# Sparse feed-forward: down product as three fp32r products, h turned earlier, weight splits dealt anew

## The reference

```python
h = silu(x @ w_gate) * (x @ w_up)          # x: 1024 x 256, h: 1024 x 1024
a = abs(h.reshape(B, S, I // 4, 4))
_, idx = top_k(a, 2)                       # of each four neighbours the two largest stay
h_sparse = h * mask
x = x + 0.5 * (h_sparse @ w_down)          # w_down: 1024 x 256
```

## Time and profile before

| | |
|---|---|
| median of 3 runs | 1663.79 us (1658.72 to 1665.37) |
| the profiled execution | 1661.38 us, span 1659.6 us |
| first sparse feed-forward | 793 to 893 us of the span |
| second sparse feed-forward | 1554 us to the end |
| PE busy, share of the span | 88% |
| DVE, ACT, POOL busy | 65%, 51%, 29% |
| mean granted TensorE clock | 0.938 of full speed |

### The profile page before, as it was taken

How to read it: one execution, slowest core, us unless ns; L and a number is a source line. 1 busy time by engine, 2 the same in 40 slices (tenths; PEclk the granted TensorE clock), 3 DMA queues, 4 the chain that set the end, 5 groups by cost and what they waited for, 6 DMA issues and landing times. The chain is left out here.

```text
span 1659.6 us, 24358 instructions
## 1 busy us (share of the span) xinstructions
PE 1454.4 (88%) x7712; PEld 1014.0 (61%) x7712; DVE 1085.8 (65%) x1948; ACT 847.5 (51%) x1206; POOL 487.5 (29%) x407
## 2 busy tenths in 40 slices
PE   3999589999999976997697887899999999998697
PEld 2566443333333344664486776788887887887586
DVE  4122499999999843121676766787877778877475
ACT  1222227777777731221433767576666675765332
POOL 1344220000000112443100104756655656565100
PEclk7999769999999976999799989999999999999799
DMA  8522211111111028222201012222222222221200
GB/s 296 145 45 45 56 27 20 26 27 27 27 27 27 5 75 299 47 47 44 92 1 39 20 38 87 90 83 89 96 77 96 76 91 93 82 91 39 76 1 26
DMA packets 83007, 111.79 MB, mean 67 GB/s; under 512 B 11904, under 2 KB 60800, under 8 KB 82912
## 3 DMA queue, kind: packets, MB, share of 16 engines
q1 hardware_dynamic: 73152, 96.05, 19.3%
q0 software_dynamic: 9376, 14.16, 4.8%
q10 hardware_dynamic: 384, 0.39, 0.1%
HBM read 89.99 MB, written 11.93 MB: 61 GB/s over the span
## 5 line engine op out<-in xcount | busy, mean ns | idle before, releaser
L923 DVE TENSOR_REDUCE attn_max_chunks<-attn_scores 128x1 f32<-128x512 f32 x488 | 305.4, 684 | 22.9 <-PE attn_scores L1174 22.8
L1085 ACT ACTIVATE attn_probs<-attn_scoresT 128x1024 f32<-128x1024 f32 x256 | 248.0, 1022 | 111.9 <-PE attn_scoresT L1190 111.6
L1174 PE MATMUL attn_scores<-attn_k_picks,attn_q_group 64*128 64x512 f32 x488 | 185.8, 461 | 11.1 <-DVE attn_max_chunks L923 2.3
L1174 PEld LDWEIGHTS attn_scores<-attn_k_picks,attn_q_group 64*128 64x128 f32 x488 | 84.7, 189 | 172.6 <-DVE attn_max_chunks L923 163.9
L1605 DVE SCALAR_TENSOR_TENSOR ssm_scan_x<-ssm_scan_proj,ssm_w_conv,ssm_scan_x 128x1023 f32<-128x1023 f32 (+2 forms) x96 | 123.0, 1282 | 81.8 <-ACT ssm_scan_x L1600 75.4
L401 DVE TENSOR_TENSOR moe_h<-moe_silu,moe_up 128x512 f32<-128x512 f32 x46 | 31.6, 688 | 189.9 <-PE moe_up L516 189.9
L1190 PE MATMUL attn_scoresT<-attn_q_group,attn_k_picks 64*128 64x512 f32 x512 | 152.2, 435 | 3.2 <-ACT attn_probs L1085 3.2
L1202 PE MATMUL attn_o<-attn_probs,attn_v_group 128*32 128x512 f32 x1024 | 137.3, 608 | 0.4 <-ACT attn_probs L1085 0.3
L62 PE MATMUL ssm_scan_proj<-ssm_xnT_hi,ssm_w_in_hi 128*128 128x512 f32 x256 | 109.4, 427 | 23.7 <-DVE ssm_scan_x L1605 21.7
L448 ACT ACTIVATE moe_silu<-moe_gate 128x512 f32<-128x512 f32 x46 | 27.5, 598 | 200.9 <-PE moe_gate L516 200.9
L286 POOL DMA_INDIRECT moe_sums<-moe_y,moe_token x46 | 72.7, 1580 | 165.7 <-DVE moe_y L410 160.0
(11 more groups left out here) (339 smaller groups left out, 3092.4 us busy)
## 6 DMA issues: line engine op xcount, KB each, us to landing
ssm_cum_all<-ssm_cums SPq DMA_DIRECT2D x32, 512.0 KB, 3.8
...
moe_sums<-main_residual SPq DMA_DIRECT2D x2, 1024.0 KB, 5.6
```

Source lines behind the costliest of these rows:

```text
L923: return nc.vector.tensor_reduce(rmaxc[:, half, place:place + 1], chunk_bank(g, n), AX_X, ALU.max).then_inc(reduced, 1)
L1085: nc.scalar.activation(probs[s % 2][:, 2 * pair:2 * pair + 2, :], st_ps[pair][:], ACT.Exp, scale=SCALE).then_inc(exp_done, 1)
L1174: nc.tensor.matmul(chunk_bank(g, n), qs[b][head_rows(j), t * P:(t + 1) * P], kz[b][head_rows(j), j % 2, c * BANK:(c + 1) * BANK], start=Tr ...
```

## The change

`down` becomes `matmul3`: 24 fp32r matmuls of 256 columns for eight fp32 ones. ACT's copy of the transposed h becomes a cast to fp32r (`hT_hi`), and DVE subtracts two halves of 512 columns (`h_low`) to get `hT_lo`. PE's list becomes `gate(t, 0)`, `up(t, 0)`, `turn_x(t + 1)`, `gate(t, 1)`, `turn_h(t - 1)`, `up(t, 1)`, `down(t - 1)`. `w_down` is split in one piece: ACT casts it between the second silu and `magnitude` of tile 0, POOL then subtracts. Of the four parts of gate and up, gate 0 goes to DVE altogether (cast and subtraction); ACT casts the other three, POOL subtracts for gate 1, DVE for both of up.

```diff
@@ sparse_ffn_layer
+        w_dn_hi = sp.sb("w_down_hi", [P, KF, D], F32R)
+        w_dn_lo = sp.sb("w_down_lo", [P, KF, D], F32R)
-        hT = sp.sb("hT", [P, KF, P])
+        hT_hi = sp.sb("hT_hi", [P, KF, P], F32R)
+        hT_lo = sp.sb("hT_lo", [P, KF, P], F32R)
...
-            eng.wait_ge(w_hi_done, w_parts.index((n, c)) + 1)
+            if (n, c) == w_parts[0]:
+                eng.wait_ge(first_hi_done, 1)
+            else:
+                eng.wait_ge(w_hi_done, w_parts.index((n, c)))
...
         @block.gpsimd
         def _(pool):
-            for n, c in w_parts:
-                if n == "gate":
-                    split_low(pool, nc.gpsimd, n, c)
+            split_low(pool, nc.gpsimd, "gate", 1)
+            pool.wait_ge(down_loaded, 64)
+            pool.wait_ge(w_dn_hi_done, 1)
+            nc.gpsimd.tensor_tensor(w_dn_lo[:], w_dn[:], f32(w_dn_hi[:]), ALU.subtract).then_inc(w_dn_lo_done, 1)
...
+            def h_low(t, c):
+                dve.wait_ge(hT_hi_done, 2 * t + c + 1)
+                own = slice(4 * c, 4 * c + 4)
+                nc.vector.tensor_tensor(hT_lo[:, own, :], hT_ps[c][:], f32(hT_hi[:, own, :]), ALU.subtract).then_inc(hT_lo_done, 1)
+
             normalize(0)
             normalize(1)
             x_low(0)
+            for k in range(KD):
+                dve.wait_ge(loaded["gate", k], 16)
+                last = nc.vector.tensor_copy(in_places(w_hi["gate"], 0)[:, k], by_place(w_raw["gate"], 0)[:, k])
+            last.then_inc(first_hi_done, 1)
+            split_low(dve, nc.vector, "gate", 0)
             split_low(dve, nc.vector, "up", 0)
             split_low(dve, nc.vector, "up", 1)
             for t in range(TT):
                 if t:
                     sparsify(t - 1)
                 product(t, 0)
+                if t >= 2:
+                    add(t - 2)
+                if t:
+                    for c in range(2):
+                        h_low(t - 1, c)
+                product(t, 1)
                 if t < LAST:
                     x_low(t + 1)
-                if t >= 2:
-                    add(t - 2)
                 if t + 2 < TT:
                     normalize(t + 2)
-                product(t, 1)
             sparsify(LAST)
             add(LAST - 1)
+            for c in range(2):
+                h_low(LAST, c)
...
                 silu(t, 1)
+                if t == 0:
+                    act.wait_ge(down_loaded, 64)
+                    nc.scalar.copy(w_dn_hi[:], w_dn[:]).then_inc(w_dn_hi_done, 1)
+                else:
+                    turned(t - 1)
                 act.wait_ge(h_done, 2 * t + 2)
                 if t:
                     act.wait_ge(sparse, t)
                 nc.scalar.activation(mag[:], h[t % 2][:], ACT.Abs).then_inc(mag_done, 1)
-                if t:
-                    turned(t - 1)
...
             def down(t):
                 if t == 0:
-                    pe.wait_ge(down_loaded, 64)
+                    pe.wait_ge(w_dn_lo_done, 1)
                 else:
                     pe.wait_ge(added, t)
                 for k in range(KF):
                     if k % 4 == 0:
-                        pe.wait_ge(hT_done, 2 * t + k // 4 + 1)
-                    last = nc.tensor.matmul(out_ps[:], hT[:, k, :], w_dn[:, k, :], start=(k == 0), stop=(k == KF - 1))
+                        pe.wait_ge(hT_lo_done, 2 * t + k // 4 + 1)
+                    last = matmul3(nc, out_ps[:], (hT_hi[:, k, :], hT_lo[:, k, :]), (w_dn_hi[:, k, :], w_dn_lo[:, k, :]),
+                                   start=(k == 0), stop=(k == KF - 1))
                 last.then_inc(out_done, 1)
 
             turn_x(0)
             for t in range(TT):
-                ups(t, 0)
+                gate(t, 0)
+                up(t, 0)
                 if t < LAST:
                     turn_x(t + 1)
-                if t >= 2:
-                    down(t - 2)
-                ups(t, 1)
+                gate(t, 1)
                 if t:
                     turn_h(t - 1)
-            down(LAST - 1)
+                up(t, 1)
+                if t:
+                    down(t - 1)
             turn_h(LAST)
             down(LAST)
```

More of the change, by code:

```diff
@@ L1347, in sparse_ffn_layer @@
         w_parts = (("gate", 0), ("up", 0), ("gate", 1), ("up", 1))
+        first_hi_done = sp.sem("first_hi_done")
         loaded = {(n, k): sp.sem(f"{n}{k}_loaded") for n in src for k in range(KD)}
@@ L1350, in sparse_ffn_layer @@
         w_hi_done = sp.sem("w_hi_done")
-        w_lo_done = {n: sp.sem(f"w_{n}_lo_done") for n in src}
+        w_lo_done = {(n, c): sp.sem(f"w_{n}{c}_lo_done") for n, c in w_parts}
         eps_done, mv_done, std_done, rstd_done = (sp.sem(n) for n in ("eps_done", "mv_done", "std_done", "rstd_done"))
@@ L1375, in split_low @@
                                          f32(in_places(w_hi[n], c)[:, k]), ALU.subtract)
-            last.then_inc(w_lo_done[n], 1)
+            last.then_inc(w_lo_done[n, c], 1)
         @block.sync
@@ L1477, in split @@
             def split(n, c):
-                if c == 0:
+                if (n, c) in (("up", 0), ("gate", 1)):
                     for k in range(KD):
@@ L1497, in turned @@
                         act.wait_ge(out_done, t)
-                    nc.scalar.copy(hT[:, 4 * c:4 * c + 4, :], hT_ps[c][:]).then_inc(hT_done, 1)
+                    nc.scalar.copy(hT_hi[:, 4 * c:4 * c + 4, :], hT_ps[c][:]).then_inc(hT_hi_done, 1)
             def silu(t, c):
@@ L1506, in _ @@
             x_high(0)
-            for n, c in w_parts:
+            for n, c in w_parts[1:]:
                 split(n, c)
@@ L1530, in turn_x, with project, gate @@
                 last.then_inc(x_turned, 1)
-            def ups(t, c):
+            def project(n, t, c, bank):
                 b = t % 2
+                if t == 0:
+                    pe.wait_ge(w_lo_done[n, c], 1)
+                for k in range(KD):
+                    cols = slice(c * BANK, (c + 1) * BANK)
+                    last = matmul3(nc, bank[:], (xT_hi[b][:, k, :], xT_lo[b][:, k, :]),
+                                   (w_hi[n][:, k, cols], w_lo[n][:, k, cols]), start=(k == 0), stop=(k == KD - 1))
+                return last
+            def gate(t, c):
                 pe.wait_ge(x_lo_done, t + 1)
@@ L1536, in ups, with up @@
                     pe.wait_ge(silu_done, 2 * t - 1 + c)
+                project("gate", t, c, gate_ps[c]).then_inc(gate_done, 1)
+            def up(t, c):
+                if t:
                     pe.wait_ge(h_done, 2 * t - 1 + c)
-                for n, bank, done in (("gate", gate_ps[c], gate_done), ("up", up_ps[c], up_done)):
-                    if t == 0:
-                        pe.wait_ge(w_lo_done[n], c + 1)
-                    for k in range(KD):
-                        cols = slice(c * BANK, (c + 1) * BANK)
-                        last = matmul3(nc, bank[:], (xT_hi[b][:, k, :], xT_lo[b][:, k, :]),
-                                       (w_hi[n][:, k, cols], w_lo[n][:, k, cols]), start=(k == 0), stop=(k == KD - 1))
-                    last.then_inc(done, 1)
+                project("up", t, c, up_ps[c]).then_inc(up_done, 1)
             def turn_h(t):
@@ L1549, in turn_h @@
                 if t:
-                    pe.wait_ge(hT_done, 2 * t)
+                    pe.wait_ge(hT_lo_done, 2 * t)
                 flat = h[t % 2][:].rearrange("p w q -> p (w q)")
```

4 lines of the change are left out of this document (3 added, 1 removed).

## The result

The changed kernel takes 1685.95 us (median of 4 runs, 1683.94 to 1687.63) beside 1664.08 for the kernel before in the same job: ratio 1.0125, 95% interval 1.0109 to 1.0141. It is slower by more than the 0.5% that can be told apart. The forecast was 1675, its range 1665 to 1681: the direction was right, the size too small, and the time lies outside the range. The profiled execution took 1683.94 us, 22.56 more than the profiled one of before (1661.38).

A forecast was written before the change was run, and what follows sets the result against it. PE alone set the 10.06 us tile before; afterwards a chain through sparsify would, at 9.75. Terms of +0.6, +2.9 and +3.3 make +6.8 us a layer, +13.6 for both: 1661.4 to 1675 us, range 1665 to 1681.

The forecast's parts named there:

- chain: Steady tiles: second product, magnitudes, sparsify and turn of h wait on each other, 9.75 us a tile; +0.6 us a layer.
- start: POOL beside DVE, cast: First tile: POOL's w_down subtraction stretches sparsify(0) by 2.5 us, ACT's cast delays magnitudes by 0.43; +2.9 us a layer.
- clock at the first turn: PE idles 4.7 us ahead of the layer's first turn of h and its clock falls; +1.5 us charged.
- clock at the last turn: PE idles 4.45 us ahead of the layer's last turn of h, clock falls to 0.50; 1.8 us charged.
- end at full clock: Last sparse to last add: level at full clock, down(7) done at 4.9 us, last add at about 5.2 as before.
- S + 2.7: Steady tile: the second product starts 2.7 us after S, the end of the previous tile's sparsify.
- `sparsify(0)` keeps 5.2 us: First tile on DVE: a sign that the prediction is wrong; it expected sparsify(0) 1.5 to 3.8 us longer than the others.
- the +0.43 for the cast: Tile 0 on ACT: casting w_down behind the second silu starts the magnitudes at 813.07 instead of 812.64.
- how the numbers follow: Closing step: forecast 0.68, range 1665 to 1681; slower 0.63, within 0.5% 0.33, faster 0.04.
- The first: Rival: chain holds, but POOL hardly slows sparsify and PE's clock does not fall; +2 a layer, 1665 us; chance 0.24.
- The second: Rival: PE stays the bound, chain shorter by say 0.3 us, seven tiles of 9.5, no clock fall; 1658 us; chance 0.05.
- The third: Rival: weight loads do not hide behind down's 24 matmuls, 5.5 us a tile; +32, near 1695 us; chance 0.03.

The follow-up runs named there:

- e5: Changed kernel with POOL's long subtraction for w_down left out (low part zero but for 8 columns); 1674.05 us, ratio 1.0046 to the kernel before.
- e6: Changed kernel plus matmuls nobody reads, 12 ahead of PE's first turn of h and 18 ahead of the last; 1673.67 us, ratio 1.0035.
- e10: Changed kernel, unchanged, run again for a second profile and time; ratio 1.0119 to the kernel before.
- e8: Kernel before the change, unchanged, run again for a second profile; ratio 0.9996.
- e11: Changed kernel without POOL's long subtraction and with 18 matmuls nobody reads ahead of the last turn of h; 1667.96 us, ratio 1.0009.
- e1: Changed kernel with POOL's subtraction for w_down cut into eight instructions of 256 columns; 1683.13 us, ratio 1.0102 to the kernel before.
- e2: Changed kernel with normalize(2) moved ahead of the second product of tile 0; 1684.76 us, ratio 1.0107 to the kernel before.
- e7: Changed kernel with fp32r down later, behind the turn; fp32 down for tiles 6 and 7; w_down's low part on DVE in four pieces; 1666.56 us, ratio 1.0012.
- e9: The changed kernel reworked: fp32r down behind the turn for tiles 2 to 5 only, w_down's subtraction on DVE, add(5) inside the last sparsify; 1660.78 us, ratio 0.9971.
- e3: Changed kernel with down as eight fp32 matmuls again, no split of w_down and no h_low, new PE order kept; 1672.40 us, ratio 1.0045.
- e4: Changed kernel with the turn of h back behind the second half, fp32r down kept a tile later, two hT buffers, add moved; 1692.75 us, ratio 1.0162.

## Why the prediction was right or wrong

Per layer, first and second, forecast against what the first profiles show:

| term | forecast | measured | from |
|---|---|---|---|
| chain | +0.6 | +0.2, +0.1 | seven steps of e5 less before |
| start: POOL beside DVE, cast | +2.9 | +3.3, +3.3 | first `sparse`, after less before |
| clock at the first turn | +1.5 | +2.6, +1.6 | seven steps, after less e5 |
| clock at the last turn | +1.8 | +2.3, +1.8 | last `add`, after less e6 |
| end at full clock | 0 | +0.1, +0.1 | last `add`, e6 less before |
| sum | +6.8 | +8.5, +6.9 | table: +8.45, +6.95 |

The second profiles (e10 less e8) give 5.6 and 3.0 for the start, 1.8 and 1.9 for the seven steps, 1.9 and 1.9 for the last `add`.

**The direction, the chain and the two falls of the clock were right.** The steady step was forecast at 9.75 and is 9.69, the second product at S + 2.7 and is at S + 2.64, `down` at 2.86 and is 2.88, and the clock fell at both turns named. e5, e6 and e11 take terms away and find the rest as it was within 0.6 us. The mechanism of the start was not right, and by the prediction's own sign (`sparsify(0)` keeps 5.2 us) wrong.

**The chain** was sized too high, even under its lower bound of +0.5: 67.8 and not 68.25, from seven times 0.06 us.

**The start term was mis-sized, by a wrong mechanism.** I read 2.12 us for 1.22 us as a slowing by 1.73, took two thirds of it on account of gaps, and said that `sparsify(0)` would be the one stretched. It kept its 5.22 us in the first profile of after, with `normalize(2)` in its place. DVE is held, not slowed in proportion: the price is what is left of POOL's 4.6 us when the first SBUF-only instruction comes, less what idle time DVE had there. It came to 3.3 where +2.5 was charged, and 3.4 to 3.7 in `sparsify(0)` of e1 and e2; the +0.43 for the cast came to nothing (e5). Minimum, median and maximum in the earlier trace rows hid this. The row of POOL that overlaps the DVE row of 1105.37 there, in the trace of before, shows it:

```profile
1105.32 1.10 POOL L2118 TENSOR_SCALAR_AFFINE_SELECT ssm_cum_all<-ssm_cum_all 128x1024 f32<-128x1024 f32 x1
```

POOL ends at 1106.42 and DVE at 1107.49, 1.07 later, not much less than the 1.22 it takes alone; wherever L2225 overlaps L2118 in this trace the distance is 1.07 to 1.09.

**The clock term** was near where it was not cut: 1.8 at the last turn, which cost 1.8 in three of the four layers and 2.3 in one. At the first turn I charged 1.5, on the ground that part of the delay is slack of PE. After the turn PE had no slack, since the next product waits for up(1, 1); it cost 1.6 to 1.8 in three layers and 2.6 in the first of the first profile. The idle times were forecast at 4.7 and 4.45 us; they were 3.31 (and 1.37 a little earlier) and 4.33.

**The step that put the time outside the range** is the last one, how the numbers follow. The layers give 15.4 us (16.2 between the second profiles, e10 less e8), 1.8 to 2.6 over the forecast's 13.6, and that alone ends at 1677 from the profiled 1661.4, or at 1679.5 from the median of before in the same job, both inside the range. The 6.5 us from there to 1685.95 lie outside the layers, where the forecast put nothing. I set the sum against that one execution and called the gap to the median +11, without allowing for the rest of the program. Its state-space layer was the shortest of thirteen profiles, and routers of 3.8 us are the short kind. Later jobs put the kernel before at 1666.2 to 1666.3. The upper end of 1681 came from the terms' bounds alone (+0.6, +1.3 and +1.2 a layer over the forecast give 1681.2; the +1.3 and +0.7 that the sentence on the range names give 1679); what differs from one execution to the next had no place in it.

**The rivals.** The first (no contention, no fall) is out by e5 and e6. The second, PE as the bound, came close in its size: PE's own step is 9.47 by e7 and e9, I had said not under 9.5, and the chain is 0.22 longer. What I named as its sign didn't work, since the steady rows name no idle time ahead of L1588 though the chain bounds; only the one at 885.89 names 0.22 us, which is 9.69 less 9.47. The third is out by 2.88 us.

**Left open.** After lies 18.8 (e10) to 21.9 us over before in the medians, its layers 15.4 to 16.2. That leaves 2.6 to 6.5 us outside the layers not accounted for; between the second profiles nothing is left. The spread of the state-space layer alone, 8.7 us, is larger, and I did not find a place for them. The same difference, median less layers, is -1.2 us in e3, -1.1 in e7, -0.1 in e6, 1.6 in e11, 1.9 in e2, 2.6 in e9, 2.9 in e1, 3.3 in e4 and 3.5 in e5. A cold start of that layer behind the slow end of the first sparse feed-forward is not borne out by this: e9 has its end at full clock and 2.6 us left, e3 the slow end and none. No run separates it cleanly. Nor is it known how often the late start of e10 and e2 comes.
